# Output projection and the following mixture norm joined into one stage, with one shared region

## What is computed

```
x = x + attn_a(layernorm(x))      # 16 heads of 16, causal, softmax, out @ Wo.T + bo
x = x + mixture(layernorm(x))     # 64 experts x 32 slots, soft dispatch and combine
x = x + attn_b(layernorm(x))      # as attn_a, without bo
x = x + mixture(layernorm(x))

def _layernorm(x, eps=1e-05):
    return (x - mean(x)) / sqrt(var(x) + eps)
```

## Time and profile before

| | |
|---|---|
| median of 3 executions | 4868.34 us (4862.49 to 4872.40) |
| profiled execution, its time | 4872.37 us |
| its span, first to last instruction | 4870.6 us |
| mean granted TensorE clock | 0.964 |
| products with the output weights, layer a, start | 1576.12 us |
| first statistics of `f_ln`, start | 1605.22 us |
| last low half of `f_ln`, start | 1648.03 us |

### The profile page before, as it was taken

How to read it: one execution, slowest core, us unless ns; L and a number is a source line. 1 busy time by engine, 2 the same in 40 slices (tenths; PEclk the granted TensorE clock), 3 DMA queues, 4 the chain that set the end, 5 groups by cost and what they waited for, 6 DMA issues and landing times. The chain is left out here.

```text
span 4870.6 us, 97833 instructions
## 1 busy us (share of the span) xinstructions
PE 4460.6 (92%) x40558; PEld 1971.9 (40%) x40558; DVE 4097.5 (84%) x4711; ACT 3124.9 (64%) x5863; POOL 1214.8 (25%) x1201
## 2 busy tenths in 40 slices
PE   5889999999999799899988999999999997998998
PEld 3322223322224465556652222232222344654566
DVE  5599998999985898778847999989998858885887
ACT  1377898888997344334433789888899964443443
POOL 2000001100002477544401000011000015774443
PEclk9699999999999799999987999999999997999999
DMA  4300000000000000220031000000000000004000
GB/s 149 76 21 8 2 15 15 8 15 8 2 2 5 18 1 1 66 74 1 0 81 65 19 4 2 15 15 15 15 2 2 2 13 9 1 1 139 10 13 13
DMA packets 73656, 112.31 MB, mean 23 GB/s; under 512 B 12389, under 2 KB 56677, under 8 KB 68965
## 3 DMA queue, kind: packets, MB, share of 16 engines
q1 hardware_dynamic: 68634, 99.95, 6.2%
q0 software_dynamic: 4608, 6.50, 1.0%
HBM read 73.70 MB, written 31.47 MB: 22 GB/s over the span
## 5 line engine op out<-in xcount | busy, mean ns | idle before, releaser
L879 DVE TENSOR_REDUCE b_att_mx<-ps 128x2 f32<-128x1024 f32 (+3 forms) x1152 | 1228.3, 1130 | 105.9 <-PE ps L732 80.5
L879 DVE TENSOR_REDUCE a_att_mx<-ps 128x2 f32<-128x1024 f32 (+3 forms) x1152 | 1228.2, 1130 | 104.4 <-PE ps L732 79.2
L836 ACT ACTIVATE a_att_pt<-ps 128x512 f32<-128x512 f32 (+3 forms) x2304 | 1146.7, 560 | 210.6 <-PE ps L768 181.0
L836 ACT ACTIVATE b_att_pt<-ps 128x512 f32<-128x512 f32 (+3 forms) x2304 | 1147.1, 560 | 208.3 <-PE ps L768 178.7
L787 PE MATMUL ps<-a_att_pt,a_v 128*17 128x256 f32 (+1 forms) x8704 | 672.6, 381 | 10.8 <-ACT a_att_osb L823 9.8
L787 PE MATMUL ps<-b_att_pt,b_v 128*17 128x256 f32 (+1 forms) x8704 | 672.0, 381 | 10.7 <-ACT b_att_osb L823 9.7
L768 PE MATMUL ps<-a_q,a_k 51*128 51x512 f16 (+3 forms) x1152 | 363.3, 370 | 0.3 <-ACT a_att_pt L836 0.2
L768 PE MATMUL ps<-b_q,b_k 51*128 51x512 f16 (+3 forms) x1152 | 362.7, 369 | 0.2 <-ACT b_att_pt L836 0.2
L713 POOL TENSOR_SCALAR_AFFINE_SELECT a_att_pt<-a_att_pt 128x512 f32<-128x512 f32 x128 | 81.3, 635 | 1123.2 <-ACT a_att_pt L836 1110.9
L713 POOL TENSOR_SCALAR_AFFINE_SELECT b_att_pt<-b_att_pt 128x512 f32<-128x512 f32 x128 | 81.4, 636 | 1122.9 <-ACT b_att_pt L836 1110.6
L768 PE MATMUL ps<-b_att_q,b_att_k 51*128 51x512 f16 (+3 forms) x1152 | 338.7, 365 | 1.1 <-ACT b_att_pt L836 0.6
(11 more groups left out here) (313 smaller groups left out, 7318.2 us busy)
## 6 DMA issues: line engine op xcount, KB each, us to landing
f_mix_ct<-in_expert_w SPq DMA_DIRECT2D x64, 256.0 KB, 5.1
g_mix_ct<-in_expert_w SPq DMA_DIRECT2D x64, 256.0 KB, 4.6
a_parts_q<-a_qkv_cut SPq DMA_DIRECT2D x24, 256.0 KB, 2.9
a_parts_k<-a_qkv_cut SPq DMA_DIRECT2D x24, 256.0 KB, 2.8
b_parts_q<-b_qkv_cut SPq DMA_DIRECT2D x24, 256.0 KB, 2.9
b_parts_k<-b_qkv_cut SPq DMA_DIRECT2D x24, 256.0 KB, 2.8
x<-in_x SPq DMA_DIRECT2D x1, 4096.0 KB, 21.8
out<-x SPq DMA_DIRECT2D x8, 512.0 KB, 2.9
```

Of the source, the lines that this page charges most:

```text
L836: act.activation(pt[:, s % PT_RING, i, 0:width], ps[:, at:at + width], ACT.Exp, scale=unscale).then_inc(pt_ready, 1)
L879: dve.tensor_reduce(mx[u % 2][:, h:h + 2, t, c], both, AX.X, ALU.max).then_inc(ring_read, 1)
```

## The change

1. `project_out` and the cut form of `layernorm` become one phase, `project_out_and_norm`, whose tags are `f_in` and `g_in`. The transposition of the attention result stands at its start as before. Then all goes by eight groups of four token tiles. VectorE's order per group g: four additions to `x`, four statistics, four aggregations, normalise group g-1, low halves of group g-2. TensorE's order: the four tiles of group g, then, from group 2 on, the eight transposes of group g-2 (`BEHIND`). ScalarE: root of g, then float16 copy and high halves of g-1. GpSimd: in layer a all 32 bias additions, then the low halves in token order.
2. Epsilon goes into the root as its bias operand, in both norms; in the mixture's norm the factor 256 goes in as well, as the root's scale 256^-2 and a bias of epsilon x 256^-2. `L320` and `L332` go away.
3. One region `m.area` of 128 x 8192 float32 is held for the whole program. It is the attention result, is overwritten by the normalised `x`, then holds `ex` and `disp` of `dispatch`, then the first of the two `ct` buffers. The output weights lie in the first part of `xacc`.
4. The transfers of `phi` are issued at the start of the joined phase, behind those of the weights and the bias row.

```diff
@@ layernorm
-                dve.wait_ge(mv_done, GT * (g + 1))
-                dve.tensor_scalar(group(ve, g), mv[:, GT * g:GT * (g + 1), 1], EPS, None, ALU.add).then_inc(ve_done, 1)
...
-                if cut:
-                    dve.tensor_scalar(group(rs, g), group(rs, g), XLN_SCALE, None, ALU.mult).then_inc(rs_done, 1)
-                    dve.wait_ge(rs_done, 2 * g + 2)
...
-                act.activation(group(sd, g), group(ve, g), ACT.Sqrt).then_inc(sd_done, 1)
+                act.wait_ge(mv_done, GT * (g + 1))
+                act.activation(group(sd, g), mv[:, GT * g:GT * (g + 1), 1], ACT.Sqrt, bias=m.eps[:, 0:1]).then_inc(sd_done, 1)
@@ project_out -> project_out_and_norm
+        @block.sync
         def _(sp):
+            sp.dma_start(w, wo.rearrange("(c p) o -> p c o", p=P)).then_inc(w_loaded, 16)
             if bias is not None:
                 sp.dma_start(brow[:, :], bias.partition_broadcast(P)).then_inc(b_loaded, 16)
+            for dst, src in loads:
+                sp.dma_start(dst, src).then_inc(loaded, 16)
+            sp.wait_ge(loaded, 16 * len(loads))
 
         @block.tensor
         def _(pe):
+            def turn(g):
+                pe.wait_ge(normed, GT * (g + 1))
+                for c in range(DC):
+                    i = DC * g + c
+                    wait(pe, low_made, i - 3)
+                    for k in range(4):
+                        mm = pe.transpose(ps[:, (i % 4) * BANK + k * P:(i % 4) * BANK + (k + 1) * P],
+                                          xln[:, 4 * g + k, c * P:(c + 1) * P], m.ident[:, :])
+                    mm.then_inc(turned, 1)
...
             for t in range(T):
                 wait(pe, added, t - 3)
...
                 mm.then_inc(made, 1)
+                if t % GT == GT - 1 and t // GT >= BEHIND:
+                    turn(t // GT - BEHIND)
+            for g in range(GROUPS - BEHIND, GROUPS):
+                turn(g)
 
         @block.scalar
         def _(act):
+            def highs(g):
+                act.wait_ge(normed, GT * (g + 1))
+                act.copy(by_token[:, GT * g:GT * (g + 1), 0, :], xln[:, GT * g:GT * (g + 1), :]).then_inc(token_high, 1)
+                for i in range(DC * g, DC * (g + 1)):
+                    dst, bank = part_of(0, i)
+                    act.wait_ge(turned, i + 1)
+                    act.copy(dst, bank).then_inc(high_made, 1)
+
             copy_part(act, act.copy, 0, filled, act_copied)
+            for g in range(GROUPS):
+                act.wait_ge(mv_done, GT * (g + 1))
+                act.activation(group(sd, g), mv[:, GT * g:GT * (g + 1), 1], ACT.Sqrt, bias=m.eps[:, 1:2],
+                               scale=XLN_SCALE ** -2).then_inc(sd_done, 1)
+                if g >= 1:
+                    highs(g - 1)
+            highs(GROUPS - 1)
...
         @block.vector
         def _(dve):
...
             copy_part(dve, dve.tensor_copy, 1, filled, dve_copied)
+            for g in range(GROUPS):
+                for t in range(GT * g, GT * (g + 1)):
+                    if bias is not None:
+                        dve.wait_ge(biased, t + 1)
+                    dve.wait_ge(made, t + 1)
+                    dve.tensor_tensor(m.x[:, t, :], out_bank(t), m.x[:, t, :], ALU.add).then_inc(added, 1)
+                for t in range(GT * g, GT * (g + 1)):
+                    dve.wait_ge(added, t + 1)
+                    dve.bn_stats(stats[:, t, :], m.x[:, t, :]).then_inc(stats_done, 1)
+                for t in range(GT * g, GT * (g + 1)):
+                    dve.wait_ge(stats_done, t + 1)
+                    dve.bn_aggr(mv[:, t, :], stats[:, t, :]).then_inc(mv_done, 1)
+                if g >= 1:
+                    normalise(g - 1)
+                if g >= 2:
+                    lows(g - 2)
+            normalise(GROUPS - 1)
+            lows(GROUPS - 2)
+            lows(GROUPS - 1)
@@ dispatch, experts_and_combine
-        ex = sb("ex", [P, EX, UNIT])
-        disp = sb("disp", [P, DISP, 2, UNIT], F16)
+        area = m.area[:, :, :].rearrange("p t d -> p (t d)")
+        ex = area[:, 0:EX * UNIT].rearrange("p (i n) -> p i n", i=EX)
+        disp = area[:, EX * UNIT:(EX + DISP) * UNIT].bitcast(F16).rearrange("p (i a n) -> p i a n", i=DISP, a=2)
...
-        ct = [sb(f"ct{i}", [P, EB, BANK]) for i in range(2)]
+        ct = [m.area[:, :, :].rearrange("p t d -> p (t d)").rearrange("p (b n) -> p b n", b=EB), sb("ct1", [P, EB, BANK])]
```

More of the change, by code:

```diff
@@ L274, in transposed, with layernorm @@
     return pe_part, copy_part
-def layernorm(nc, m, ps, tag, xln, xlnT, by_token=None, loads=()):
-    cut = by_token is not None
+def layernorm(nc, m, ps, tag, xln, xlnT):
     GT = 4
@@ L296, in group @@
             return t[:, GT * g:GT * (g + 1)]
[L298 to L309, removed]
         @block.vector
@@ L366, in _ @@
                     root(g + 1)
[L367 to L369 removed]
                 for i in range(DC * g, DC * (g + 1)):
[L371 to L373 removed]
+                    if i % 2 == 0:
                         act.wait_ge(filled, i + 1)
[L375 to L383, removed]
+                        act.copy(xlnT[:, i % DC, g * BANK:(g + 1) * BANK], ps[:, (i % 4) * BANK:(i % 4 + 1) * BANK]).then_inc(act_copied, 1)
         @block.tensor
         def _(pe):
[L387 removed]
+            pe_part(pe, m.ident[:, :], lambda eng, n: eng.wait_ge(normed, n), filled, act_copied, dve_copied)
 def load_head(eng, qt, kt, r, head, parts_q, parts_k, loaded):
@@ L883, in _, with project_out_and_norm @@
                     dve.tensor_reduce(mfull[u % 2][:, :, :], mx[u % 2][:, :, :, 0:g + 1], AX.X, ALU.max).then_inc(m_full, 1)
-def project_out(nc, m, ps, tag, attn, wo, bias):
+def project_out_and_norm(nc, m, ps, tag, attn, wo, bias, w, xlnT, by_token, loads):
+    GT = 4
+    GROUPS = T // GT
+    BEHIND = 2
     with phase_of(nc, tag) as (ctx, sem, sb):
         attnT = sb("attnT", [P, DC, N])
-        w = sb("w", [P, DC, D])
-        brow = sb("brow", [P, D])
-        w_loaded, b_loaded = sem("w_loaded"), sem("b_loaded")
+        brow = sb("brow", [P, D]) if bias is not None else None
+        stats, mv = sb("stats", [P, T, 6]), sb("mv", [P, T, 2])
+        sd, rs = sb("sd", [P, T]), sb("rs", [P, T])
+        xln = attn
+        w_loaded, b_loaded, loaded = sem("w_loaded"), sem("b_loaded"), sem("loaded")
@@ L897, in project_out, with group, out_bank, part_of @@
         block = ctx.enter_context(nc.Block())
+        def group(t, g):
+            return t[:, GT * g:GT * (g + 1)]
+        def out_bank(t):
+            return ps[:, (4 + t % 4) * BANK:(4 + t % 4) * BANK + D]
+        def part_of(part, i):
+            g, c = divmod(i, DC)
+            rows = P - (c == DC - 1)
+            return xlnT[0:rows, part, c, g * BANK:(g + 1) * BANK], ps[0:rows, (i % 4) * BANK:(i % 4 + 1) * BANK]
         @block.sync
         def _(sp):
-            sp.dma_start(w[:, :, :], wo.rearrange("(c p) o -> p c o", p=P)).then_inc(w_loaded, 16)
+            sp.dma_start(w, wo.rearrange("(c p) o -> p c o", p=P)).then_inc(w_loaded, 16)
@@ L932, in _, with normalise @@
[L932 to L937, removed]
+            def normalise(g):
+                dve.wait_ge(sd_done, g + 1)
+                dve.reciprocal(group(rs, g), group(sd, g)).then_inc(rs_done, 1)
+                dve.wait_ge(rs_done, g + 1)
+                for t in range(GT * g, GT * (g + 1)):
+                    dve.tensor_scalar(xln[:, t, :], m.x[:, t, :], mv[:, t, 0:1], rs[:, t:t + 1],
+                                      ALU.subtract, ALU.mult).then_inc(normed, 1)
@@ new lines, in lows @@
+            def lows(g):
+                for i in range(DC * g, DC * (g + 1)):
+                    dst, bank = part_of(1, i)
+                    dve.wait_ge(high_made, i + 1)
+                    dve.tensor_tensor(dst, bank, part_of(0, i)[0], ALU.subtract).then_inc(low_made, 1)
+            copy_part(dve, dve.tensor_copy, 1, filled, dve_copied)
+            for g in range(GROUPS):
+                for t in range(GT * g, GT * (g + 1)):
[6 more added lines that the diff above has]
+                    dve.bn_stats(stats[:, t, :], m.x[:, t, :]).then_inc(stats_done, 1)
+                for t in range(GT * g, GT * (g + 1)):
+                    dve.wait_ge(stats_done, t + 1)
[4 more added lines that the diff above has]
+                    lows(g - 2)
@@ L1491, in build, with attention_layer, mixture_layer @@
                      (t["a_WqT"], t["a_WkT"], t["b_WqT"], t["b_WkT"]))
-        def attention_layer(tag, layer, wq, wk, wv, wo, bias, denom_bias):
+        def attention_layer(tag, layer, wq, wk, wv, denom_bias):
             parts_q = nc.dram_tensor(f"{tag}_parts_q", (3, D, N), F16).ap()
             parts_k = nc.dram_tensor(f"{tag}_parts_k", (3, D, N), F16).ap()
[L1496 to L1507, removed]
+            with ExitStack() as kept:
+                v = kept.enter_context(nc.sbuf_tensor(f"{tag}_v", [P, T, HEADS, VW], F32))
```

(14 more changed lines are left out.)

32 lines of the change are left out of this document (15 added, 17 removed).

## The result

| | before | after |
|---|---|---|
| median, executions | 4869.49 us, 4 | 4827.51 us, 4 |
| lowest to highest | 4862.49 to 4872.40 | 4824.78 to 4832.44 |
| profiled execution, its time | 4872.37 us | 4824.78 us |

The account below looks back on a forecast made before the run. Two successive stages, bound by TensorE and then VectorE, each leave the other engine half idle. Savings of 20.5 (g), 17.7 (f) and 2.4 (plain norms) sum to 40.6 us, giving a median of 4828 us, range 4815 to 4847.

Parts of the forecast that it names:

- Where the time lies; VectorE bounds the new stage: Output projection and cut norm, 72.60 us a layer, become one stage bound by VectorE at 5.73 us a step.
- TensorE, ScalarE and the waits are hidden: In a steady joined step TensorE works 4.5 of 5.73 us, ScalarE under 2.5, and nobody waits for either.
- The normalisation waits for GpSimd: In the joined stage, normalisations meeting GpSimd wait: 1.95 us lost at each layer's end, 2.8 more in layer f.
- The rival of no conflict: In the joined stages normalisation never waits for GpSimd: 6.7 us more won, 4821 us; chance 0.16.
- The price of the bias: Layer f only: the first normalisations fall among GpSimd's 32 bias additions and lose four turns of at most 0.69, 2.8 us.
- The upper bound of 5.6: Layer f: most the bias additions could cost, if both of the first two groups of normalisations meet them.
- Epsilon in the plain norms: Dropping the epsilon instruction saves 0.15 us eight times per plain norm: 1.2 us each, 2.4 for two.
- Transfers and region: Start of the joined phase: w lands in about 8 us, before it is needed; the shared region costs 0.
- The sign that dispatch and combine must keep their times: Four stages of unchanged work; other times there, with their buffers in the region, would show the forecast wrong.
- The late bias row: Layer f: a bias row landing late would cost the other half of the 5.6 us.
- the rivals with a low clock: TensorE's clock falls within the joined stage: in part, chance 0.14, or throughout, chance 0.05.
- The 4847 at the top of the range: Slow end of the forecast range, the half-low case of TensorE's clock in the joined stages: 4847 us.

Follow-up runs that it names:

- behind1: The changed kernel with TensorE's transposes one group behind the products instead of two: 4877.97 us, ratio to before 1.0019.
- pause: The changed kernel with GpSimd waiting on its own semaphore between the 32 bias additions: 4832.0 us, ratio to before 0.9926.
- region_alone: The kernel before with only the shared region added, stages left apart: 4867.09 us, ratio to before 1.0000.

## Why the prediction was right, and where not

- *Where the time lies; VectorE bounds the new stage.* Right. A steady step was forecast at 5.73 us and is 5.58. Aggregation 0.28 instead of 0.35 and reciprocal 0.18 instead of 0.21 make most of it; statistics, normalisation and low halves are as forecast, 1.31, 1.30 and 1.20. Layer g: 52.1 forecast, 50.8 measured.
- *TensorE, ScalarE and the waits are hidden.* Right, with 0.43 and 0.35 us of TensorE's own waiting a step. `behind1` shows that the distance of two groups is what this rests on.
- *The normalisation waits for GpSimd.* Right, but it was an assumption: no row has the normalisation beside GpSimd, so none shows the 1.95 and the 2.8 that the sum takes from it. It rested on the multiplication by 256, 1.99 instead of 0.17, and on the select's 1.26 beside L220. The runs showed 8.47 and 2.11 us for a median of 0.41. The rival of no conflict (4821) is refuted. At the end of the stage 1.95 was forecast for each layer and 1.70 measured.
- *The price of the bias.* This term was mis-sized: "Four turns of at most 0.69 are 2.8 us", measured 8.05, and about 1 more for the low clock behind it; f took 60.0 us for the forecast's 54.9. The step that failed is "Where the two engines alternate". It was taken from L1389, beside which GpSimd waits on its own semaphore before every addition. The bias additions had no such wait. Put in (`pause`), it gives the alternation, at 1.4 and 1.5 us a group. The upper bound of 5.6 was built on alternation as well, and so too low. By the forecast's own times a stop to the end of the run would have been 1592.1 - 1585.6 = 6.5 us; the 1.7 by which the additions began later (5.97 less 4.24) make up the rest within 0.2. That second part is an estimate; no run tests it alone. The forecast's second normalisation at 1592.6 follows from neither case: its steps give 1590.2 without the stop and 1593.0 with 2.8.
- *Epsilon in the plain norms.* 1.2 forecast, 1.8 measured: between the aggregations and the next instruction 0.28 is left of 0.39, and the bound of 0.17 an instruction left out that wait. That the root would take 0.1 longer with its bias operand came true: 0.297 instead of 0.205, hidden.
- *Transfers and region.* Right for w, which was not waited for, and for the region within the noise: `region_alone` is at 1.0000. The sign that dispatch and combine must keep their times came out mixed, 385.5 and 388.1 for 386.5 and 383.7 in dispatch, which is within what it varies. The late bias row was named, but not counted: it landed 2.0 us later and lengthened the stop.
- *The clock.* In the steady steps of g it stayed at 0.98, and in f it was down only behind the stop (0.51, and 1.00 from 1590 on). In the last 8 us of each layer, with 16 transposes left, it was 0.50 and 0.51, as in the old end that the forecast took over; the full clock there, which the lower bound of the range allowed for, did not come about. Nor did the rivals with a low clock; `behind1` shows a related case, idle time (3.59) and then a low clock (0.50). The 4847 at the top of the range stands for half of the steady steps at half the clock, an estimate; no run shows what a step would then take. The nearest is `behind1`, 9.4 us a step at 0.86.
- *The sum.* Forecast 20.5 + 17.7 + 2.4 = 40.6. The stages give 21.7 + 12.6 + 3.6 = 37.9, and the medians 42.0, with 32 to 49 in the interval. So the 4827.5 beside 4828 is partly luck: f was 5 us worse, g and the norms 2.5 better, and the rest is the spread of the executions. Against before as it was measured again (4867.59) the changed kernel is 40.1 us lower.

## What to carry to other kernels

Two stages bound by different engines can be joined when the follower stays far enough behind: here two groups hid TensorE's waits wholly (0.43 and 0.35 us a step), while with one TensorE waited 3.59 us a step and all that was won, 50 us, was lost. Before joining, look for what now stands beside what: an instruction of VectorE that was never beside a run of GpSimd's lost here all that was left of the run (8.05 us for the group), not a turn of 0.69. Work that nobody waits for, such as the bias, belongs in a stage where the trace shows that engine waiting.

## What the runs showed of the hardware

- A VectorE normalisation (float32 in SBUF, two per-partition operands) begun during back-to-back GpSimd additions took 8.47 us: the rest of the addition that was running and the 12 behind it. With GpSimd waiting on its own semaphore between the additions, VectorE got in after each, four instructions in 2.87 us. A semaphore wait that was already met did not let it in: beside two low halves in 4.21 us one normalisation took 2.38. The 2.11 us of the last group in g (changed kernel) are the rest of one GpSimd instruction; the 8.47 reaches over 13 in a row and the 2.38 over two.
- Such a wait stands in the profile as busy time of the waiting instruction. VectorE shows 9.30 of 9.30 us busy in that stretch; only the duration of the line's slowest instruction, 8467 ns for a median of 406, gives it away.
- The low clock lengthened the stop in f: TensorE's eight transposes took 1.97 us behind it (granted clock 0.51) and 1.09 in the steady steps (0.98).
